# A two-layer transformer in fp32: each bank of a first-attention maximum read and released on its own, and an exponential of a constant placed behind the last Gelu

## What is computed

```python
x = x + attn0(layernorm(x))   # 8 heads of 64, keys and values from a latent of 64
x = x + ffn0(layernorm(x))    # silu(w1 x) * (w2 x), gelu(h1 .), gelu(h2 .), w3; hidden 1024
x = x + attn1(layernorm(x))   # 16 heads of 16, rotary positions
x = x + ffn1(layernorm(x))    # silu(gate) * up, down; hidden 768

def attn0(x):
    q, kv = x @ Wq.T, x @ Wkv_down.T
    k, v = kv @ Wk_up.T, kv @ Wv_up.T
    s = einsum("bqhd,bkhd->bhqk", q, k) * 64 ** -0.5
    return einsum("bhqk,bkhd->bqhd", softmax(s), v) @ Wo.T
```

## Time and profile before

| | |
|---|---|
| median of 3 runs | 2405.14 us (2404.36 to 2409.79) |
| the profiled execution | 2402.36 us, its span 2400.6 us |
| TensorE busy | 2331.3 us, 97% of the span |
| TensorE in 40 equal slices of the span | 6, 9 and 8 tenths busy, then 9 or more in every one |
| VectorE, ScalarE, GpSimd busy | 1504.9, 1342.5, 1046.5 us |
| first attention | from 0 to about 789 us |
| L720 reductions 128 x 1024 | 164, mean 1218 ns |
| L722 and L723, 128 x 512 each | 84 and 84, mean 685 and 679 ns |
| chain of work that ended last | TensorE 62%, ScalarE 2%, VectorE 1% |

### The profile page before, as it was taken

The page is one execution under the profiler, slowest core; times in us unless marked ns, Lnnn a source line. Parts: engine busy times, 40 slices in busy tenths (PEclk is TensorE's granted clock), DMA queues, the critical chain, the costliest instruction groups (busy, mean ns, idle before and its releaser), DMA issues.

```text
span 2400.6 us, 39029 instructions
## 1 busy us (share of the span) xinstructions
PE 2331.3 (97%) x15265; PEld 1449.8 (60%) x15265; DVE 1504.9 (63%) x1938; ACT 1342.5 (56%) x1783; POOL 1046.5 (44%) x674
## 2 busy tenths in 40 slices
PE   6989999999999999999999999999999999999999
PEld 4545555555555788888888887444444444444588
DVE  6877777787784224322222223779989989989364
ACT  3555555554444444444444443478778778777743
POOL 1656776766677346556556556130000000000354
PEclk8999999999999999999999999999999999999999
DMA  2111321221212455565565556433333323322232
GB/s 61 63 69 54 98 79 56 98 65 61 73 44 69 149 167 181 176 196 184 172 197 185 173 188 201 128 90 80 88 79 72 86 77 75 90 79 55 61 121 80
DMA packets 156836, 259.04 MB, mean 108 GB/s; under 512 B 37004, under 2 KB 97292, under 8 KB 156300
## 3 DMA queue, kind: packets, MB, share of 16 engines
q1 hardware_dynamic: 156652, 256.53, 35.7%
HBM read 206.52 MB, written 60.68 MB: 111 GB/s over the span
## 4 chain that ended last, share of the span: by engine, by line
PE 62%; ACT 2%; DVE 1%; DMA 1%; issue 1%; SPq 1%; POOL 0%; POOLq 0%
PE m_R L129 46%; PE m_O L129 11%; PE m_X L129 4%; ACT m_P L1704 1%; DMA m_K<-bounce_k 1%; PE m_X L226 1%; ACT m_OS L1711 1%; DVE m_mraw L1853 0%; SPq L1562 0%; PE m_X L2067 0%; DVE m_ln_x L205 0%; PE m_R L226 0%; DMA inverses<-m_rinv 0%; DVE m_ln_stat L183 0%; SPq L1589 0%
## 5 line engine op out<-in xcount | busy, mean ns | idle before, releaser
L1853 DVE TENSOR_REDUCE m_mraw<-m_R 128x2 f32<-128x1024 f32 x512 | 622.6, 1221 | 71.1 <-PE m_R L129 57.6
L1704 ACT ACTIVATE m_P<-m_R 128x1024 f32<-128x1024 f32 x512 | 523.5, 1025 | 149.6 <-PE m_R L129 149.2
L589 ACT ACTIVATE a_P<-a_S 128x1024 f32<-128x1024 f32 x256 | 248.7, 1023 | 214.5 <-PE a_S L129 213.6
L129 PE MATMUL m_O<-m_P,m_V 128*17 128x256 f32 x4096 | 330.1, 394 | 4.5 <-ACT m_P L1704 2.6
L888 POOL TENSOR_TENSOR a_accp<-a_accp,a_P 128x1024 f32<-128x1024 f32 x96 | 251.9, 2624 | 15.3 <-ACT a_P L589 6.1
L1958 POOL TENSOR_TENSOR m_act0l<-m_xf,m_act0h 128x512 fp32r<-128x512 f32 x128 | 164.8, 1290 | 210.6 <-ACT m_xf L1766 111.2
L129 PE MATMUL a_O<-a_P,a_V 128*64 128x512 f32 x1024 | 247.7, 605 | 4.4 <-ACT a_ON L597 4.4
L129 PE MATMUL m_R<-m_act0h,wt 128*128 128x512 f32 x640 | 251.5, 393 | 0.0
L129 PE MATMUL m_R<-m_act0l,wt 128*128 128x512 f32 x640 | 250.4, 391 | 0.0
L720 DVE TENSOR_REDUCE a_mraw<-a_X 128x2 f32<-128x1024 f32 x164 | 199.7, 1218 | 79.6 <-PE a_X L129 79.5
L129 PE MATMUL m_R<-m_Q,m_K 64*128 64x512 f32 x800 | 200.6, 498 | 2.3 <-DVE m_mraw L1853 2.0
(11 more groups left out here) (251 smaller groups left out, 4235.0 us busy)
## 6 DMA issues: line engine op xcount, KB each, us to landing
wt<-wcopy SPq DMA_DIRECT2D x176, 512.0 KB, 3.4
m_K<-bounce_k SPq DMA_DIRECT2D x96, 128.0 KB, 5.4
m_ln_x<-x SPq DMA_DIRECT2D x23, 512.0 KB, 4.0
a_tile<-in_L_ffn_tiles SPq DMA_DIRECT2D x22, 512.0 KB, 4.5
wcopy<-in_L_ffn_tiles SPq DMA_DIRECT2D x22, 512.0 KB, 5.2
x<-xres SPq DMA_DIRECT2D x78, 128.0 KB, 3.2
m_Q<-bounce_q SPq DMA_DIRECT2D x150, 64.0 KB, 2.2
xres<-x SPq DMA_DIRECT2D x64, 128.0 KB, 2.6
```

Source lines behind the costliest of these rows:

```text
L129: return pe.eng.matmul(out, lhsT, rhs, start=start, stop=stop, skip_group_check=True)
L589: act.eng.activation(P[n % NP][:, :, :], psS[n % 2][:, :, :], ACT.Exp, scale=SCALE).then_inc(s_exp)
L1704: act.eng.activation(P[h % 4][:, :, :], pair(key)[:, :, :], ACT.Exp, scale=SCALE).then_inc(R.free(key))
L1853: dve.eng.tensor_reduce(mraw[u % 2][:, at, :], pair(key)[:, :, :], AX.X, ALU.max).then_inc(R.free(key))
```

## The change

In `attention_a`, a maximum becomes two ring entries, ("max", n, 0) and ("max", n, 1), of one bank each; the order and the banks stay as they were. TensorE waits for the earlier users of both banks ahead of the first of the two matmuls, as before, but each matmul now counts up its own bank. VectorE reads each bank by an instruction of its own, behind its own wait, and releases it with that instruction. In `ffn_attention_ffn`, ScalarE computes the exponential of a tile of the constant -0.5 (128 x 4) behind the last Gelu, into a tile `ready` that nothing reads.

```diff
-            out += [("max", n)] if early_banks(n) is None else []
+            out += [("max", n, h) for h in range(NH)] if early_banks(n) is None else []
...
-            out += [("max", n), ("max", n + 1)] if n < STEPS else []
+            out += [("max", n + i, h) for i in range(2) for h in range(NH)] if n < STEPS else []
...
-        X = Ring(p, "x", 3, x_order(), double=("max",))
+        X = Ring(p, "x", 3, x_order())
...
-            return psX[:, (X.slot(("max", n)) + h) % 3, :]
+            return bank(("max", n, h))
...
-                    dve.wait_ge(*X.filled(key))
-                    first = X.slot(key)
-                    if first < 2:
-                        dve.eng.tensor_reduce(mraw[u % 2][:, t, :], psX[:, first:first + 2, :], AX.X, ALU.max).then_inc(X.free(key))
-                    else:
-                        dve.eng.tensor_reduce(mraw[u % 2][:, t, 0:1], max_bank(n, 0), AX.X, ALU.max)
-                        dve.eng.tensor_reduce(mraw[u % 2][:, t, 1:2], max_bank(n, 1), AX.X, ALU.max).then_inc(X.free(key))
+                    for h in range(NH):
+                        key = ("max", n, h)
+                        dve.wait_ge(*X.filled(key))
+                        dve.eng.tensor_reduce(mraw[u % 2][:, t, h:h + 1], bank(key), AX.X, ALU.max).then_inc(X.free(key))
                 if t == NT - 1:
...
-                            dve.wait_ge(*X.emptied(("max", k)))
+                            for h in range(NH):
+                                dve.wait_ge(*X.emptied(("max", k, h)))
...
-                    pe.wait_free(X, key)
+                    for h in range(NH):
+                        pe.wait_free(X, ("max", n, h))
...
                     ins = mm(pe, max_bank(n, h), Qh[u % 3][rows, 128 * q:128 * q + 128], kt[rows, 512 * kh:512 * kh + 512])
-                ins.then_inc(X.full(key) if early_banks(n) is None else s_early)
+                    if early_banks(n) is None:
+                        ins.then_inc(X.full(("max", n, h)))
+                if early_banks(n) is not None:
+                    ins.then_inc(s_early)
...
+        ready = p.sb("ready", [128, 4])
...
                     if key[0] not in ("gate", "up"):
                         leave(key)
+                    if key == ("hidden", NB - 1, 1, MT - 1):
+                        act.wait_ge(norm.s_half, 1)
+                        act.eng.activation(ready[:, :], norm.minus_half[:, :], ACT.Exp)
```

More of the change, by code:

```diff
@@ L709, in reduce @@
             def reduce(n):
-                u, t, key = n // NT, n % NT, ("max", n)
+                u, t = n // NT, n % NT
                 if t == 0 and u >= 2:
@@ L945, in maxima @@
             def maxima(n):
-                u, key = n // NT, ("max", n)
+                u = n // NT
                 q, kh = divmod(n % NT, 2)
```

## The result

The changed kernel takes 2395.5 us in the median of 8 runs (2391.4 to 2398.9); the kernel before, on the same chip, 2404.75 us (2401.8 to 2409.8). The ratio is 0.9957, with a 95% interval of 0.9948 to 0.9966: 10.3 us gained, between 8.2 and 12.5; the forecast was 8.8. (The quotient of the two medians is 0.9962. The ratio isn't worked out from the medians, and the two can differ by 0.001 in the experiments too.) The profiled run of the changed kernel took 2395.5 us with a span of 2393.7, so the two profiled spans are 6.9 us apart.

The account below looks back on a forecast made before the run. TensorE, busy for 97% of the span, was taken as the bound, so only its waits count. Gains of 6.3 us (banks) and 2.5 us (table load) sum to 8.8: 2393.6 us from the profiled 2402.36, or 2396.3 from the median; range 2391 to 2402.

Parts of the forecast that it names:

- Part 2: Second attention's start: table load hidden behind the last Gelu gains 2.5 us, 1.3 of load and 1.2 of clock.
- part 1: First attention: maxima reduced and released one bank at a time gain 6.3 us, between 2 and 8.3.
- two rivals to it: Second attention's start: clock falls all the same, 2397.5 us, chance 0.18; table load does not hide, 2398.8 us, chance 0.02.
- five second maxima: Second maximum of a turn, 48.99 to 151.46 us: five stalls gain 2.3 us from a first bank released early.
- six transposes and latents: Six stalls at 167.46 to 545.90 us needing only a maximum's first bank, released early: 3.3 us gained.
- four first maxima: First maximum of a turn, 592.50 to 706.60 us: four stalls gain 2.1 us from a first bank released early.
- stalls that need both banks: Eleven TensorE stalls, six behind sums and five behind a q: no gain, each 0.1 us longer, 1.1 us lost.
- given back: TensorE's earlier request meets a VectorE not caught up: three quarters of part 1 lost, 2403.1 us; chance 0.15.
- near places: 37 weight loads that waited for a reduction while the matmul was not late: a few become stalls, 0.7 us lost.
- 30 stalls: TensorE's listed waits for reductions L720, 17 times, 13.2 us, and L723, 9 times, 4.4 us, plus four transposes.
- price of the split: VectorE: two narrow reductions cost 0.07 us more than a wide one, for 164 splits 11 us, where it has idle time.
- slower rival: VectorE's reductions become the bound, from about 0.14 us a split: 10 us lost, 2.5 won, 2412.6 us; chance 0.05.

Follow-up runs that it names:

- e2: The kernel before with only the small exponential behind the last Gelu added; 2.9 us less than before (-0.2 to 5.8).
- e1: The changed kernel without the small exponential; 7.2 us less than the kernel before (4.3 to 10.1).
- e3: The kernel before, maxima outside the two early banks reduced in two narrow steps, both banks released by the second; 5.3 us slower (2.2 to 8.7).
- f2: The kernel before with GpSimd's additions at t = 2, 3, 6 and the merging one over 8 columns only; 14.0 us less (10.8 to 17.1).
- f3: e3 with the same GpSimd additions over 8 columns as f2; 6.5 us slower than f2.
- e7: The changed kernel, but the first narrow reduction waits until both banks are written; 6.3 us less than the kernel before (4.1 to 8.7).
- f1: e6 with each of GpSimd's additions over 128 x 1024 cut into two halves; 2381.1 us, 26.5 us less than the kernel before.
- e6: The changed kernel with VectorE's tile chore behind the second reduction and the query's difference in turns with j = 0; ratio 0.9953 to the kernel before.
- f4: The changed kernel with the same GpSimd additions over 8 columns as f2; 14.2 us less than f2.
- e4: The changed kernel with a VectorE memset of 128 x 1 behind each pair of narrow reductions; 2397.2 us, ratio 0.9952 to the kernel before.
- e8: The changed kernel with a VectorE memset of 128 x 200 behind each pair of narrow reductions; ratio 0.9971 to the kernel before.

## Why the prediction was right, point by point

The total was right by more than it deserved. Part 2 was right in both terms. In part 1 the bank that comes early does what was predicted where only one bank is needed. But 6.7 us of waits grew or are new where 1.1 were counted, and 2.5 us came from places that I had put down as a loss. That these two nearly cancel is luck.

**Part 2: right.** Forecast 2.5, between 1.3 and 3.0; the traces give 2.7 and the times of e2 2.9. The table load went off the path (1.4, forecast 1.3), one short wait stayed (0.33, forecast 0.4 to 0.5), and PEclk is 1.00 behind it where it was 0.52 (1.3, forecast 1.2). Of the two rivals to it, neither happened. The first exponential of e1, as that before, follows the load at once; the drain of 1.38 us that the Trainium skill adds ("ScalarE: Activation LUTs", section "What ACT_TABLE_LOAD costs") shows in neither, nor in the changed kernel, where the small exponential begins 0.01 us behind the load. The clock's part has no fixed size: behind the same wait of 1.75 us the kernels e3, f2 and f3 lost more.

**The gain of the stalls that need one bank: right in mechanism, 8.3 us forecast, 6.5 measured.** The five second maxima gave 2.9 us (forecast 2.3), the six transposes and latents 2.8 (3.3), the four first maxima 0.7 (2.1) and the two rows 0.1 (0.6). The maximum of the earlier trace rows waited 0.85 us, and 0.37 after: 0.48 gained, forecast 0.55. Three of the first maxima are like it; the one at 621.38, 0.67 us, grew to 1.30 (at 617.61), since VectorE's addition ahead of it began 0.35 us behind one of GpSimd's and took 3.13 us, where it had been 0.83 behind and took 2.65. The transposes of the earlier trace rows 1.00, and 0.43 after: 0.57, forecast 0.56 (my list of signs said that this wait and that of the earlier trace rows would vanish, against my own sum, which left 0.44 and 0.30). The second maximum of the earlier trace rows has no wait any more, nor has the query projection behind it, for which I had kept 0.49: between 41 and 114 us no listed wait for a reduction is left. Narrow reductions start 0.60 us apart, as in the earlier trace rows.

**The stalls that need both banks: wrong.** I let them stand, each 0.1 us longer. Some shrank, since the first half now starts before the second bank is written, a point I named and then put at nothing: 1.81 us of the earlier trace rows became 1.31, where 1.8 to 2.0 were forecast. e7 measures the early start at about 4 us. Others grew or are new: 0.34 us at 138.17 became 1.11 at 137.09, 1.45 at 575.78 became 1.95 at 570.33, and 1.40 at 731.64 wasn't there. So the waits for `a_mraw` are 18.5 us and not about 10. At each of these places one of VectorE's long steps stands behind one of GpSimd's: whether it takes 1.2 us or 3 depends on which engine begins first, and where GpSimd is first, a VectorE that comes earlier only waits longer (at 134.55 us before, 1.15 behind GpSimd's, the step took 2.33; at 132.67 after, 0.39 behind, 3.08). So the rival "given back" is in part what happened: it counted 2 us of new stalls and 6.7 grew or are new. What it lacked is this mechanism, by which VectorE gives time back not for having too much to do but for waiting for GpSimd. How much of the 6.7 us is GpSimd's isn't measured; f1 comes nearest to it, with listed waits for reductions 9.5 us below those of e6.

**The near places: wrong in sign.** I counted 0.7 us lost. The list of waits leaves out what is below about 0.15 us, and the step "30 stalls" took it for complete. Behind an output projection, TensorE before, then VectorE's reduction that it waits for, in unit 11:

```profile
283.43 0.28 PE L129 MATMUL a_X<-a_wo,a_osp0h 128*128 128x256 f32 x1
283.68 0.23 PE L129 MATMUL a_X<-identr,a_mneg 128*8 128x128 f32 x1
...
282.41 1.21 DVE L720 TENSOR_REDUCE a_mraw<-a_X 128x2 f32<-128x1024 f32 x1
```

and after:

```profile
280.68 0.28 PE L129 MATMUL a_X<-a_wo,a_osp0h 128*128 128x256 f32 x1
280.80 0.22 PE L129 MATMUL a_X<-identr,a_mneg 128*8 128x128 f32 x1
...
279.71 1.28 DVE L720 TENSOR_REDUCE a_mraw<-a_X 128x1 f32<-128x512 f32 x2
```

The transpose starts 0.25 us behind the projection's last matmul before, and 0.12 after: it needs the first bank of the reduction that ends at 283.62, and that bank now comes at 279.71 + 0.68 = 280.39. No row carries a wait. Going through the starts of all matmuls against the shortest distance that the same pair of instructions has elsewhere, I find 17 such places at the transposes of `a_mneg` before, 2.6 us together, and 0.1 us or less in the changed kernel and in e1; in e3 they are 4.0 us, and the unlisted waits before maxima are 0.6 longer than before. That is 2 of the 9.6 us that e3's trace loses by the feed-forward layer, and it goes on without GpSimd's additions: 2.9 us in f2, 4.2 in f3, 0.1 in f4. The weight loads' waits, 63 places against 21, had pointed there; I read them as places with something to lose.

**The price of the split: too small, and the threshold wrong.** Costs of 1.1 + 0.2 + 0.7 = 2.0 us were forecast; e3 puts the split alone at 5.3 (2.2 to 8.7). The slower rival should have set in at 0.14 us of VectorE's time a split. e4 is at 0.13 and costs nothing that can be measured, e8 at 0.3 and costs some 3 us. Neither the 0.07 us nor the 0.14 that follows from the rule of the drain mattered as VectorE's time. (In the Trainium skill the same section, "The DRAIN you can't avoid" of "VectorE: DVE Perf Modes", also says that an operation which isn't held starts earlier; the pairs here do, 0.60 us apart.) In the first attention e3 differs from e4 in that both banks wait for the second narrow reduction, so I take the longer path of TensorE through a reduction for e3's cost; no run varies that length alone.

**The sum.** Part 1: forecast 6.3; e1 gives 7.2 (4.3 to 10.1). In the traces the first attention ends 2.8 us earlier in the changed kernel, 5.5 in e1 and 3.5 in e4, which have the same instructions on TensorE there, and 0.2 earlier in e2, which has those of before. The forecast of 6 for that point is met by none of the three; their mean is 3.9. What follows to the second attention adds 1 to 2 us, which is the clock and no term of mine.

## What to carry to other kernels

Where an engine on the way to the bottleneck stands behind the long operations of another that nobody waits for, cut those into pieces: it then waits for a piece. Here, with e6's order, that was worth 10 to 15 us, as much as the change itself or more, at about 0.2 us of GpSimd's time a cut (1482 + 1286 ns for L883's 2571). A list of waits has a floor; compare start distances of equal pairs of instructions, and take weight loads that waited as a sign that something stands there. And an activation table can be loaded by a dummy operation in idle time, which pays twice if the wait it removes is one behind which the clock falls.

## What the runs showed of the hardware

- One VectorE step of 128 x 1024 with both inputs in SBUF takes 1.2 us when it begins 0.1 us before one of GpSimd's, and up to 3.4 behind one, by how long GpSimd's still has to run. A cast with one input in SBUF (0.86 us in e6) was held up too, 2.86 us at 566.13; the memsets (59 and 225 ns each) and the narrow reductions from PSUM never were (694 ns at the most among 496).
- TensorE's granted clock fell behind some waits of 1.7 us and more and not behind others: to 0.85 and 0.72 in 568 to 576 us of the changed kernel behind 1.95 us, but not behind 2.13 us at 158.38 and 1.77 at 641.71 in the same trace, nor behind the 1.81 us of the earlier trace rows. Behind the 1.75 us at the second attention's start it fell in five kernels of five. Low stretches came at other places too (198 and 1741 us in e3, 157 us in f2, 158 and 380 in f3), in e3 at 198 with no long wait ahead. The times of one kernel spread with the clock: e3's fastest run (2405.6 us) had a mean granted clock of 0.995, its slowest (2418.9) 0.991. Whether kernels with more waits spread more isn't shown.
- VectorE's narrow reductions overlap by 0.08 us even across a wait that is already fulfilled (1.27 to 1.29 us for two that last 0.68 to 0.69). Starting on one bank while TensorE writes the next doesn't lengthen them: 682 ns mean in the changed kernel, 685 and 679 before.
